# A graph network of two spline convolutions and an attention layer on one core: the MLP's last pass is moved behind the convolutions, and x is gathered further ahead

## The reference

```python
h = relu(layernorm(x));  x = x + conv2(relu(conv1(h)))      # the two spline convolutions
h = relu(layernorm(x));  x = x + attention(h)

# a convolution: each edge mixes four of 25 matrices W by its two attributes
msg  = sum_over_4_corners(basis * (h[src] @ W[corner]))      # per edge
agg  = segment_max(msg, dst)                                 # 0 for a node without incoming edges
conv = agg + h @ root + bias                                 # per node

# attention: d comes from a small MLP on three coordinates of each edge, not on x
d = gelu(layer_norm(gelu(layer_norm(coords @ Wd1 + bd1)) @ Wd2 + bd2))
logits = (h @ W1)[dst] - (h @ W2)[src] + d
out = segment_softmax_weighted_sum(logits, (h @ W3)[src] + d)   # over the edges of each dst
```

## Time and profile before

| | us |
|---|---|
| median of 3 runs | 1812.44 (1810.86 to 1816.27) |
| the profiled execution, its own time | 1817.89 |
| its span, first to last instruction | 1815.4 |
| PE, DVE, POOL, ACT busy | 83%, 79%, 68%, 39% of the span |
| MLP before its last pass | about 37 to 107 |
| MLP's last pass | about 107 to 131 |
| conv 1 | about 131 to 676 |
| first boundary | 676 to 699 |
| conv 2 | 699 to 1258 |
| second boundary | 1258 to 1275 |
| attention | 1275 to 1815 |

### The profile page before, as it was taken

How to read it: one execution, slowest core, us unless ns; L and a number is a source line. 1 busy time by engine, 2 the same in 40 slices (tenths; PEclk the granted TensorE clock), 3 DMA queues, 4 the chain that set the end, 5 groups by cost and what they waited for, 6 DMA issues and landing times.

```text
span 1815.4 us, 33798 instructions
## 1 busy us (share of the span) xinstructions
PE 1501.9 (83%) x7834; PEld 998.9 (55%) x7834; DVE 1430.6 (79%) x2753; ACT 709.0 (39%) x1766; POOL 1240.6 (68%) x1232
## 2 busy tenths in 40 slices
PE   3978888888888975999999999995777766777764
PEld 2855566665666653777777777774343433333332
DVE  5258999999999973999999999995576666666764
ACT  3563333333333321233333333331455555554553
POOL 5035777777777757777767776760577777777776
PEclk9988999999999996999999999998899999998998
DMA  8973444444444434888777778773333333333330
GB/s 137 156 83 81 101 104 104 102 105 105 101 107 101 106 70 135 236 234 231 230 224 227 222 225 228 226 233 93 77 72 77 68 68 68 72 76 68 68 74 19
DMA packets 408182, 232.02 MB, mean 128 GB/s; under 512 B 306089, under 2 KB 382058, under 8 KB 408146
## 3 DMA queue, kind: packets, MB, share of 16 engines
q1 hardware_dynamic: 311834, 151.97, 31.2%
q0 software_dynamic: 44864, 65.52, 16.8%
q10 hardware_dynamic: 51448, 14.14, 6.2%
HBM read 141.68 MB, written 92.64 MB: 129 GB/s over the span
## 4 chain that ended last, share of the span: by engine, by line
PE 33%; POOL 11%; issue 9%; DMA 4%; ACT 3%; DVE 3%; SPq 0%; POOLq 0%; DVEq 0%; ACTq 0%
PE bank L1007 17%; POOL gath L609 6%; POOL out_dram L616 5%; PE bank L1000 3%; DMA gath<-M,gidx 3%; PE bank L1049 2%; PE bank L1066 2%; PE bank L1128 2%; PE bank L1038 2%; PE bank L1027 1%; PE bank L1058 1%; PE bank L1075 1%; PE bank L1147 1%; DMA arena<-T 1%; DVE arena L1623 1%
## 5 line engine op out<-in xcount | busy, mean ns | idle before, releaser
L1007 PE MATMUL bank<-Wk,arena 128*128 128x320 f32 (+1 forms) x2352 | 656.7, 465 | 57.5 <-ACT arena L786 57.5
L1007 PEld LDWEIGHTS bank<-Wk,arena 128*128 128x128 f32 (+1 forms) x2352 | 328.4, 190 | 304.0 <-issue 223.0
L609 POOL DMA_INDIRECT gath<-T,gidx x392 | 386.8, 987 | 148.9 <-issue 111.8
L786 ACT ACTIVATE arena<-bank 128x256 f32<-128x256 f32 (+1 forms) x392 | 169.6, 433 | 321.2 <-PE bank L1000 320.6
L609 POOL DMA_INDIRECT gath<-M,gidx x196 | 210.9, 1076 | 119.9 <-issue 54.9
L616 POOL DMA_INDIRECT T<-srow,sidx x196 | 215.0, 1097 | 79.8 <-issue 57.0
L609 POOL DMA_INDIRECT gath<-in_x_dram,gidx x196 | 197.8, 1009 | 71.8 <-issue 59.1
L1406 DVE TENSOR_TENSOR arena<-bank,A 128x320 f32<-128x320 f32 x392 | 191.9, 489 | 65.6 <-PE bank L1007 58.2
L616 POOL DMA_INDIRECT out_dram<-srow,sidx x196 | 199.0, 1015 | 61.4 <-issue 60.8
L1000 PE MATMUL bank<-ident,arena 128*128 128x128 f32 x980 | 172.0, 275 | 31.2 <-DVE arena L1386 31.2
L1000 PEld LDWEIGHTS bank<-ident,arena 128*128 128x128 f32 x980 | 124.2, 141 | 62.2 <-issue 31.2
(11 more groups left out here) (213 smaller groups left out, 2659.6 us busy)
## 6 DMA issues: line engine op xcount, KB each, us to landing
arena<-T SPq DMA_DIRECT2D x48, 816.0 KB
T<-arena SPq DMA_DIRECT2D x96, 272.0 KB
T<-zero ACTq DMA_DIRECT2D x1, 13281.2 KB, 103.6
B<-arena SPq DMA_DIRECT2D x49, 256.0 KB
arena<-B SPq DMA_DIRECT2D x49, 256.0 KB, 3.7
arena<-in_x_dram SPq DMA_DIRECT2D x48, 256.0 KB, 4.1
out_dram<-arena SPq DMA_DIRECT2D x48, 256.0 KB
begins_cut<-begins_d SPq DMA_DIRECT2D x49, 128.5 KB, 3.4
```

Source lines behind the costliest of these rows:

```text
L609: pool.indirect_dma_start(out=gath[slot][:, j, k, 0:width], out_offset=None, in_=table, in_offset=bass.IndirectOffsetOnAxis(gidx[slot][:, ...
L786: act.activation(ZT[j // 2][:, first:first + chunks, :], bank[j % 2][:, 0:chunks * P], ACT.Relu)\
L1007: return pe.matmul(bank[2 + r][:, 0:KO], ZT[q][rows, chunk, :], Wk[n - 1][rows, weights].rearrange("p k o -> p (k o)"), start=start, stop= ...
```

## The change

Three parts.

**1. The MLP's last pass** no longer runs before conv 1. Its groups 0 to 12 run in the first boundary, 13 to 24 in the second. POOL's spread becomes an ACT copy of the same shape. The indices of conv 2's first gathers are written before ACT waits for the scatters. PE's wait for the end of the pass before conv 1 becomes a wait for the second root (`s_root`).

**2. Conv 2's node pass** reads slots 1 and 2 only (544 KB a group instead of 816; the runs in HBM are 544 bytes, one per node, instead of 6528 per partition). For a node without incoming edges slot 0 is zero; the others' rows are written over later. DVE's addition becomes an ACT copy, placed between ACT's evacuations 803 and 786 of a step.

**3. Conv 1's gathers of x** run eleven groups ahead in twelve small buffers (three in each of the four `gath` tiles). The loops of POOL, ACT and DVE in conv 1 now hold 12 steps in a body; PE's and SP's stay at 4.

```diff
+XS = 12
+    LAST_PASS = ((0, 13), (13, MG))
+        xrows = [gath[i // per].rearrange("p t e c -> p (t e c)")[:, i % per * TPG * C:(i % per + 1) * TPG * C]
+                 .rearrange("p (t c) -> p t c", c=C) for i in range(XS)]
+        xidx = [gidx[i // per][:, i % per * TPG:(i % per + 1) * TPG] for i in range(XS)]
-        def each(eng, step, before, after, n=G, ahead=2, first=0):
+        def each(eng, step, before, after, n=G, ahead=2, first=0, unroll=UNROLL):
 # SP, conv 2
-                    sp.dma_start(nt[n.parity][0:p], rows).then_inc(t["nload"][n.parity], 16)
+                    sp.dma_start(nt[n.parity][0:p], rows[:, :, U:ROW]).then_inc(t["nload"][n.parity], 16)
 # POOL, conv 1
-                if (g + 3).within(G):
-                    n = g + 3
+                if (g + XS - 1).within(G):
+                    n = g + XS - 1
                     wait(pool, s["gidx"], n)
-                    wait(pool, s["ecen"], n - 2)
+                    wait(pool, s["ecen"], n - XS)
+                    wait_fill(pool, s["gathered"], n - SLOTS, 16 * TPG)
-                    gather(n.parity, a["x"], 0, C, s["gathered"])
+                    for j in range(TPG):
+                        pool.indirect_dma_start(out=xrows[slot][:, j, :], ...)
-            pool.wait_ge(s_rstd, 3)
-            each(pool, spread_rstd, 0, 0, MG)
-            each(pool, step, 1, 1, ahead=3)
+            each(pool, step, XS - 1, 1, ahead=XS - 1, unroll=XS)
 # ACT
-            for g in (0, 1):
+            for g in range(XS):
                 gidx1(Group(None, g))
+            def last_pass(first, last):
+                act.preload_act_table_set("gelu_and_others")
+                def step(g):
+                    if (g + 2).within(last, first):
+                        e = g + 2
+                        wait(act, m2["turn"], e - 2)
+                        act.activation(rstd_rows[e.parity], mst[:, 1, ...].broadcast_to([P, MT, C]), ACT.Copy)
+                    if g.within(last, first):
+                        wait(act, m2["norm"], g)
+                        act.activation(chunk_of_DT(g), chunk_of_DT(g), ACT.Gelu, ...)
+                each(act, step, 2, 0, last, first=first)
+                        wait_fill(act, s["nload"], g, 16)
+                        wait(act, s["npe"], g - 1, "nt")
+                        act.activation(nh[:, :, :], nt[g.parity][:, :, 0:C], ACT.Copy).then_inc(s["xn"].sem, 1)
             conv(1)
-            scatter_done(act, cs[1])
             for g in range(SLOTS):
                 gidx2(Group(None, g))
+            act.wait_ge(s_rstd, 3)
+            last_pass(*LAST_PASS[0])
+            scatter_done(act, cs[1])
             conv(2)
 # PE, and DVE alike
-            end_of(pe, m2["norm"], MG)
+            pe.wait_ge(s_root, 2)
             conv(1)
+            last_pass(*LAST_PASS[0])
             conv(2)
+            last_pass(*LAST_PASS[1])
 # DVE
-                each(dve, step, 2, 1)
+                each(dve, step, 2, 1, unroll=XS if n == 1 else UNROLL)
```

More of the change, by code:

```diff
@@ L71, in times @@
             return per * self.off + plus
-        return self.h * (UNROLL * per) + (per * self.off + plus)
+        return self.h * (self.unroll * per) + (per * self.off + plus)
     def slot(self, slots):
@@ L395, in conv_sems @@
                 s.update(signals("c1", "gidx sidx rowid esum ecen esq evar nsum ncen nsq nvar root a0r"))
-                s["gathered"], s["scattered"] = pair("c1_gathered"), [sem(f"c1_scattered_{i}") for i in range(SLOTS)]
+                s["gathered"], s["scattered"] = [sem(f"c1_gathered_{i}") for i in range(SLOTS)], [sem(f"c1_scattered_{i}") for i in range(SLOTS)]
                 s["xstore"] = pair("c1_xstore")
@@ L639, in step @@
                     scatter(n, s, T1, third_bound, U)
[L641 to L646, removed]
-                                 .broadcast_to([P, MT, C])).then_inc(m2["spread"].sem, 1)
-            pool.wait_ge(s_rstd, 3)
-            each(pool, spread_rstd, 0, 0, MG)
-            each(pool, step, 1, 1, ahead=3)
+            each(pool, step, XS - 1, 1, ahead=XS - 1, unroll=XS)
             scatter_done(pool, cs[1])
@@ L840, in step @@
                             .then_inc(s["row"].sem, 1)
-                each(act, step, 3, 1, ahead=3)
+                each(act, step, 3, 1, ahead=XS if n == 1 else 3, unroll=XS if n == 1 else UNROLL)
             act.wait_ge(s_w, WEIGHTS)
@@ L976, in _, with last_pass, step @@
             each(pe, step, 1, 1, MG)
-            def step(g):
-                wait(pe, m2["norm"], g - 2)
-                wait(pe, m2["spread"], g)
-                for q in range(PAIRS):
-                    tr = pe.transpose(bank[g.parity][:, q * P:q * P + P],
-                                      rstd_rows[g.parity][:, 2 * q:2 * q + 2, :].rearrange("p t c -> p (t c)"),
-                                      ident[:, :])
-                tr.then_inc(m2["turn"].sem, 1)
-            each(pe, step, 0, 0, MG)
+            def last_pass(first, last):
+                def step(g):
+                    wait(pe, m2["norm"], g - 2)
+                    wait(pe, m2["spread"], g)
+                    for q in range(PAIRS):
+                        tr = pe.transpose(bank[g.parity][:, q * P:q * P + P],
+                                          rstd_rows[g.parity][:, 2 * q:2 * q + 2, :].rearrange("p t c -> p (t c)"),
+                                          ident[:, :])
+                    tr.then_inc(m2["turn"].sem, 1)
+                each(pe, step, 0, 0, last, first=first)
             def conv(n):
@@ L1340, in _, with last_pass, step @@
             end_of(dve, m1["keep"], MG)
-            def step(g):
-                wait(dve, m2["turn"], g)
-                V_.tensor_tensor(chunk_of_DT(g), chunk_of_DT(g), bank[g.parity][:, :], ALU.mult)\
-                    .then_inc(m2["norm"].sem, 1)
-            each(dve, step, 0, 0, MG)
+            def last_pass(first, last):
+                def step(g):
+                    wait(dve, m2["turn"], g)
+                    V_.tensor_tensor(chunk_of_DT(g), chunk_of_DT(g), bank[g.parity][:, :], ALU.mult)\
+                        .then_inc(m2["norm"].sem, 1)
+                each(dve, step, 0, 0, last, first=first)
             def conv(n):
```

84 lines of the change are left out of this document (42 added, 42 removed).

## The result

The changed kernel took **1781.85 us** (median of 4, 1779.58 to 1782.96), the kernel before 1814.14 in the same comparison (4 runs, 1810.86 to 1816.27): ratio 0.9822, 95% interval 0.9802 to 0.9842. Forecast were 1790.5 us, range 1780 to 1801: inside the range, but outside the likeliest case's own range (1786 to 1795). The span fell from 1815.4 to 1781.2 us, by 34.2; the sum had 21.9.

A forecast was written before the change was run, and what follows sets the result against it. Bounds by stage: DVE in conv 1, PE in conv 2, POOL in the attention, transfers in two holes between. Terms summed to -21.9 us on the profiled 1817.9, so 1796.0, or 1790.5 against the median 1812.4; range 1780 to 1801.

The forecast's parts named there:

- likeliest case: Whole kernel: the forecast of 1790.5 us, own range 1786 to 1795, given a chance of 0.50.
- The start: Before conv 1: starting without the last pass gives -22.6 us, a dropped sqrt table load -0.6.
- A step of conv 2: Conv 2's steady steps: DVE loses 0.68 us of work, but PE has the bound, so 0.
- Conv 2's first step: Conv 2's start: of PE's 2.60 us wait for DVE's node sum, 1.6 go; bounds 0 and -3.
- The last load: Conv 2's last node load: lands sooner with two thirds of the bytes, -2.5 us; bounds -3.0 and -1.4.
- The second boundary: Between conv 2 and the attention: the last pass's remaining groups delay PE's first turn, +3.1 us; bounds 0 and +5.
- The long loops: Conv 1: DVE's 540-instruction body fetches at two returns, +5.2, fewer returns -0.7; taken +4.5 us, bounds -0.7 and +8.
- The gathers: Conv 1's first steps: DVE's waits of 0.47 and 0.85 us for x go, -1.3 us.
- no fetch: Rival, conv 1: the long loops cost nothing, -0.7 instead of +4.5, giving 1785.3 us; chance 0.20.
- the zeroing: Rival: early conv 1 meets the zeroing of T1, late node loads, start 13 instead of 22 us earlier, 1799.7; chance 0.10.
- late in conv 2: Rival: ACT's copy ahead of the evacuation makes PE stand in each conv 2 step, 30.9 us, to 1821; chance 0.05.
- the holes: Rival, both boundaries: the last pass overruns each hole by 3 us more, giving 1796 us; chance 0.14.

The follow-up runs named there:

- run 1: Kernel before with only conv 2's node pass changed (two slots loaded, ACT copies, DVE's addition gone); ratio 0.9933, 1803.9 us.
- run 2: Changed kernel, but DVE instead of ACT hands over conv 2's node rows, on the smaller load; ratio 0.9873 of the kernel before.
- run 7: Kernel before with conv 1 on DVE written straight out, nothing else; ratio 1.0005 of the kernel before.
- run 5: Changed kernel with 18 instead of 13 groups of the last pass in the first boundary; ratio 0.9795 of the kernel before.
- run 10: Changed kernel with 20 identity transposes on PE at the end of each part of the last pass; ratio 0.9809 of the kernel before.

## Why the prediction was right and where it was wrong

- **The start, -23.2**: -23.4. Right, step by step.
- **A step of conv 2, "DVE loses 0.68 us, but PE has the bound: 0"**: this step failed. It is -0.13 a step, -5.9 in all (runs 1 and 2). PE had the bound, but not all of its busy time was work: one operation a step waited 0.1 us for DVE, too short to be marked. The term was put at nothing from a busy share alone. Its bounds should have come from start-to-start times: in before the order of PE's rows is the same in each step, but its second step took 10.96 us and the last but one 10.84, against 11.08 and more in nearly all others.
- **Conv 2's first step, -1.6**: the mechanism was right, the size not: -3.5. The bound of -3 named the clock; the product behind the wait of the earlier trace rows had run 1.33 us longer at the lower clock, and that row was there to be read. Part of it is chance, through the clock: in run 7, whose conv 2 is before's code, PE waited 2.02 us at this place, the clock stayed up and the products took 3.26, so that this stretch of the ledger was 16.87 us instead of 18.45.
- **The last load, -2.5**: -1.3. Runs 1 and 2 had 1.7 and 1.3, with or without ACT's copy, so it is the load. How much is less sure: all kernels with the smaller load lie between 11.67 and 12.67 us, but with the larger one before had 13.96 and run 7 had 15.61.
- **The second boundary, +3.1**: +0.3. The pass does cost that much: the kernel with the node pass alone, which has no pass there, needed 49.35 us to POOL's first scatter, the changed kernel 52.02, so +2.7. Before needed 51.69: its clock fell back after PE's first operations (0.57 in 1285 to 1289). Run 7, with before's code here, had no such fall after its rise and needed 49.34. So some 2.4 us came back through the clock, whose rise differs between executions of the same code; not forecastable from the rows, though inside the bounds.
- **The long loops, +4.5**: +3.4, two stalls of 2.3 us less 0.26 given back at once, less 0.7 for returns. Right, also in that it takes place at the return on DVE and costs in full.
- **The gathers, -1.3**: -1.6. Right; but that a loop on DVE costs 0.20 us in every step, and that POOL has nothing to spare, was missed. The steps after the loop, at 10.62, brought 1.9 unforeseen.
- **The rivals**: "no fetch" refuted by the stalls and the instruction packets; the zeroing did not disturb conv 1 (no wait on a node load there); ACT was never late in conv 2 (PE waited for its copy only once, 1.7 us at the last load); the holes were not overrun with 13 groups.

Sum of the misses: -5.9 (conv 2's steps) - 1.9 (its first step) - 1.9 (conv 1's late steps) - 2.8 (second boundary) - 1.1 (loops) + 1.2 (last load) and small ones make the 12.3 us between -21.9 and -34.2. That the time still fell into the range, 1.9 us from its lower end, is luck in part: that end had been set wide of "no fetch" (1785.3), which was refuted, and not for conv 2's steps, which no bound and no rival allowed to get faster.

## To carry to other kernels

An engine that is busy 100% of a stage can still be waiting: compare its start-to-start times with those of a run in which the suspected partner's work has been moved away. When two engines are within 2% of the same step time, relieving one can show nothing; here, in conv 1, straight code on DVE (0.20 us a step) and a long lead for POOL's gathers were each worth 0 and together 12 us. And a loop body on DVE of about 360 or 540 instructions cost about 2.3 us at each return, so either keep it short or write it straight out.

## What the runs showed of the hardware that I had not expected

- A DVE loop of about 360 instructions stalled 2.3 to 2.5 us at each return, one of 540 2.3 (2.5 in runs 2 and 5), one of 191 not. The 49 steps written straight out never did.
- A loop cost DVE 0.20 us in a step of 10.8 besides its returns, with register instructions in it that straight code lacks, shown partly as a wait for another engine.
- After a wait of 2.4 to 2.6 us on PE in conv 2's first step the granted clock was down, and the twelve products behind it took 4.6 to 4.9 us instead of 3.25: in before and runs 2 and 10. It isn't so after every such wait: after 2.02 us at the same place in run 7 they took 3.26, and after the 3.03 us at conv 2's end ten took 2.72.
- From POOL's first scatter of the attention to the end it took 510.4 us in before, 510.6 in the changed kernel, but 508.0, 508.1 and 507.7 in runs 1, 2 and with 16 groups, and between 507.2 and 510.9 in the others, whose attention is the same code. These 3.7 us between executions are in no theory here; it is why the ledgers go by landmarks.
